# One chunk of every seventeenth group gathered row by row by SyncE in two graph passes

## The chip, the cores and the metric

The kernel runs on one core of one Trainium2 chip. The metric is device time in microseconds (us); the median of three runs before is 9730.03 us. Its engines are TensorE (PE; its weight loads are PEld), VectorE (DVE), ScalarE (ACT), GpSimd (POOL) and SyncE (SP); a q behind a name is the engine's sequencer.

## What is computed

Four graph layers over one graph of 6250 nodes and 100000 edges (`dst` sorted), each followed by a layer norm. Layers 1 and 2 concern us: per edge a score is made from a row of the source node and a row of the destination node, the scores are normalised by a softmax over the edges of each destination, and the weighted source rows are summed per destination.

```python
# layer 1 (relational attention, 8 heads)
kt = einsum('nhi,thij->tnhj', k, relation_att)[edge_type, src]
e = (q[dst] * kt).sum(-1) * relation_pri[edge_type] * scale
a = softmax over the edges of each dst (e)
vt = einsum('nhi,thij->tnhj', v, relation_msg)[edge_type, src]
agg = segment_sum(a[..., None] * vt, dst)
# layer 2 (additive attention, 4 heads, with self loops)
e = leaky_relu(x_l[src] + x_r[dst], 0.2)
logits = einsum('ehc,hc->eh', e, att)
out = segment_sum(softmax(logits)[:, :, None] * x_l[src], dst)
```

## The kernel before, in words

Edges are sorted by destination into 832 chunks of 128 edges (one edge to a partition), `G = 4` chunks to a group, `GROUPS = 208`. `read_order` (L734) reads the sorted list from DRAM as rows of 104 partitions, turns it on TensorE and writes the SBUF lists of indices `by_dst.other` (source node) and `by_dst.typed` (type times `NPD`, plus source node): one column of 128 indices for a chunk. SP then stores the segment breaks, and the block ends when the store has landed.

`softmax_pass` (L1361) runs once for each of layers 1, 2 and 3; the change touches the first two calls (L3266, L3283). It has no scheduler: the work of every engine is written out in one order, and semaphores link them.

- POOL (L1495 to L1507) gathers the source rows: one indirect DMA a chunk, 128 rows of 1024 bytes in layer 1 (`related`) or 528 bytes in layer 2 (`left_table`), into `rows`, a ring of `ring = lag + 1` groups. Here `lag = wg + 6`, and a window is `wg` groups: 4 in layer 1, 8 in layer 2. From the ring's second round on, group n waits for `weighed >= n - ring + 1`, that is, until DVE has weighed group n - ring. So POOL may fill group n once DVE has finished its turn n - 1.
- DVE (L1698 on) takes turns n = 0, 1, 2, ... In turn n it marks the one-hots of group n (helper line L140), pairs group n - 2 with its destination rows (L1788 in layer 1, L1791 in layer 2), reduces the pair to scores (L1814), weighs group n - lag (L1877) and adds the sums of group n - lag - 2 into `total` (L1694). In some turns of each window it also takes the steps of the running maximum: L1760, L1798 to L1845, and the waits for `small`, which PE makes (L1765, L1831). It is first in, first out: a wait in turn n holds all of this back.
- PE turns the one-hots (L1569), fetches destination rows by matmul (L1582; in layer 2 it also adds the gathered rows, and so waits for them there) and makes the sums (L1600, L1610).
- SP (L1474 to L1494) loads the breaks at the start of a pass (`brk`, L1479: 32 DMAs in layer 1, 64 in layer 2), and has nothing more until the pass ends (in layer 1 `reload` at L1492).

`load_blocks` (L129) loads several numbers from one partition of SBUF into registers of an engine, by one TENSOR_LOAD.

```python
pool.wait_ge(weighed if at else scored, n - ring + 1 + (NBLK // G if ringed else 0))
nc.gpsimd.indirect_dma_start(rows[:, s, g, :], None, table, ...).then_inc(got[s], 16)
dve.wait_ge(got[t % ring], (t // ring + 1) * 16 * G)
```

Of the kernel before, what the change touches and what calls it, by code (L numbers as in the profile page):

```python
# [48 lines left out]
AFTER = NSLOT - E  # L49
assert TU * QU == CU and RING * G == 64 and NBLK < (RING - 2) * G  # L50
# [683 lines left out]
def read_order(nc, k, table, o, breaks, fields, name, stack=None, shared=None):  # L734


    with ExitStack() as own:
# [7 lines left out]
        end = sb("end", [1, P], BF16)  # L745
        outs = [out for _, out in fields] + [o.begins]
# [614 lines left out]
def softmax_pass(nc, k, o, index, table, row, head, values_at, spread, att, peaks, total, reload, loops, wg, name, beside=(),  # L1361
                 ringed=False):
# [21 lines left out]
    with ExitStack() as ctx:  # L1384
# [73 lines left out]
        kept = sem("kept")  # L1458
        block = ctx.enter_context(nc.Block())
# [15 lines left out]
        def _(sp):  # L1475
# [11 lines left out]
            if beside:  # L1487
                sp.wait_ge(kept, 16 * len(beside))
            if reload is not None:
# [6 lines left out]
        def _(pool):  # L1496
            for n in range(GU if ringed else GROUPS):
# [5 lines left out]
                for g in range(G):  # L1503
# [52 lines left out]
        def _(pe):  # L1556
# [4 lines left out]
            for n in range(slots):  # L1561
# [10 lines left out]
                if 0 <= t < GROUPS:  # L1572
# [6 lines left out]
                    if att is not None:  # L1579
                        pe.wait_ge(got[t % ring], (t // ring + 1) * 16 * G)  # L1580
# [81 lines left out]
        def _(dve):  # L1662
# [33 lines left out]
            for n in range(slots + 1):  # L1696
# [3 lines left out]
                if n >= GROUPS + 2:  # L1700
                    add_sums(n - lag - 2)
                if n < GROUPS:
# [65 lines left out]
                if 0 <= t < GROUPS:  # L1768
# [6 lines left out]
                    else:  # L1775
                        dve.wait_ge(got[t % ring], (t // ring + 1) * 16 * G)
# [1356 lines left out]
def graph_network(nc, a, out):  # L3133
    k = Shared()
    k.semaphores = []
    with ExitStack() as ctx:
# [27 lines left out]
        by_src.free = sb("src_free", [1, 2 * P], I32)  # L3164
        by_dst.typed = sb("dst_typed", [P, CH + SPARE], I32)
# [11 lines left out]
        with ExitStack() as sort:  # L3177
# [51 lines left out]
            with unblocked as dense:  # L3229
                def tmp(name, shape, dt=F32):  # L3230
# [31 lines left out]
                       [(1, by_dst.other), (2, by_dst.typed), (0, by_dst.place)], "dst_read")  # L3262
            free_semaphores(nc, k)
        with ExitStack() as layer:
            total = layer.enter_context(nc.sbuf_tensor("l1_total", [P, NBLK - 1 + G, D + HEADS1], F32))
            softmax_pass(nc, k, by_dst, by_dst.typed, related.rearrange("t n f -> (t n) f"), 2 * D, D // HEADS1, D,  # L3266
                         k.x, None, False, total, (k.x[:], x_home), None, 4, "l1_pass")
# [6 lines left out]
        with ExitStack() as layer:  # L3274
            def tmp(name, shape, dt=F32):
# [8 lines left out]
                         None, (left, loop_scores, k.x[:], bias2[:]), 8, "l2_pass")  # L3284
# [47 lines left out]
```

## Time and profile before

| | us |
|---|---|
| median of 3 runs (lowest, highest) | 9730.03 (9727.62, 9735.21) |
| the profiled execution, its own time | 9737.26 |
| its span | 9735.5 |
| pass of layer 1, first gather to last | 5188.4 to 6251.5 |
| pass of layer 2, first gather to last | 6429.9 to 7481.0 |
| busy: PE, DVE, ACT, POOL | 6374.2, 6539.5, 2118.1, 6993.0 |

Times within the span count from its start. An engine's busy time leaves out its sequencer's work, which a view of SP or of a line shows as SPq, DVEq and so on. Idle time is put down to what ended it; "issue" is idle time in which the engine waited for nothing that the profile shows.

### The profile page before, as it was taken

What the parts mean: (1) busy time and instruction counts of PE and PEld (TensorE: products, weight loads), DVE (VectorE), ACT (ScalarE), POOL (GpSimd) and SP (SyncE); (2) the same over time, 40 slices, a digit from 0 to 9 for tenths busy, and PEclk for the clock granted to TensorE, in tenths of its full rate; (3) what the DMA queues carried; (4) which work ended last, traced back from release to release, by engine and by line L of the source; (5) the groups of instructions that cost most, each with busy time, mean ns of one, the idle gap of its engine ahead of it and who ended that gap; (6) DMA issues with size and microseconds to landing.
All of it is one profiled execution on the core that took longest, in us unless ns stands there. A gap on an engine that the chain in (4) does not pass through costs nothing. (4 is left out here: it accounts for less than half of the span.)

```text
span 9735.5 us, 171552 instructions
## 1 busy us (share of the span) xinstructions
PE 6374.2 (65%) x37681; PEld 5551.4 (57%) x37682; DVE 6539.5 (67%) x22695; ACT 2118.1 (22%) x6216; POOL 6993.0 (72%) x7418
## 2 busy tenths in 40 slices
PE   6777655547666577639404666767776688876666
PEld 5666544436655566634204666556675578766665
DVE  7555566668777777736305888877777666667777
ACT  5222100001111111112101222232222222223333
POOL 7777777767777777777776777547775577767775
PEclk7555555556666655569756888889999665667777
DMA  0000012122212212234303333222222322223333
GB/s 25 2 2 2 18 53 52 53 61 53 53 53 55 57 53 53 53 77 146 100 2 86 104 104 104 87 47 55 55 55 55 100 54 54 54 72 108 108 108 97
DMA packets 436037, 614.74 MB, mean 63 GB/s; under 512 B 176561, under 2 KB 312069, under 8 KB 435109
## 3 DMA queue, kind: packets, MB, share of 16 engines
q0 software_dynamic: 257024, 486.93, 19.6%
q1 hardware_dynamic: 178305, 119.49, 4.3%
q8 instruction: 183, 3.00, 0.1%
q10 hardware_dynamic: 292, 3.41, 0.1%
q14 instruction: 233, 1.91, 0.1%
HBM read 520.17 MB, written 89.19 MB: 63 GB/s over the span
## 5 line engine op out<-in xcount | busy, mean ns | idle before, releaser
L1179 PE MATMUL hop_sums<-hop_rows,hop_weighted 128*128 x4992 | 1152.1, 403 | 1053.2 <-SPq L1315 674.4
L1128 POOL DMA_INDIRECT hop_rows<-hops,k_src_gather x1568 | 1483.3, 946 | 486.8 <-issue 477.6
L1179 PEld LDWEIGHTS hop_sums<-hop_rows,hop_weighted 128*128 128x128 f32 x4992 | 989.6, 295 | 1158.8 <-issue 1158.7
L1505 POOL DMA_INDIRECT l_pass_rows<-left_table,k_dst_other x832 | 796.2, 957 | 433.2 <-issue 244.6
L1505 POOL DMA_INDIRECT l_pass_rows<-related,k_dst_typed x832 | 788.6, 948 | 308.6 <-issue 238.7
L1505 POOL DMA_INDIRECT l_pass_rows<-key_table,k_src_gather x784 | 744.3, 949 | 365.9 <-issue 234.8
L2000 POOL DMA_INDIRECT l_weigh_rows<-row_table,l_weigh_ring x832 | 790.0, 949 | 297.9 <-issue 213.1
L728 POOL DMA_INDIRECT src_sorted<-src_scatter_records,src_scatter_places x784 | 753.1, 961 | 260.4 <-issue 188.2
L1355 POOL DMA_INDIRECT dst_sorted<-rec,dst_places x768 | 752.8, 980 | 237.2 <-issue 237.2
L1128 POOL DMA_INDIRECT hop_rows<-in_x,k_src_gather x784 | 742.4, 947 | 249.0 <-issue 238.7
L1213 DVE TENSOR_SCALAR hop_weighted<-k_numbers,k_src_place,src_weight 128x128 f32<-128x128 f32 x2496 | 850.1, 403 | 15.7 <-issue 8.7
L1521 ACT CAST l_pass_onehot_t<-l_pass_turned 128x512 f32<-128x512 bf16 x624 | 365.7, 586 | 2158.6 <-PE l_pass_turned L1569 2110.8
L1600 PE MATMUL l_pass_sums<-l_pass_zero 128*128 128x272 bf16 (+1 forms) x1210 | 235.7, 279 | 465.2 <-DVE l_total L1694 322.0
L1582 PE MATMUL l_pass_own<-l_right,l_pass_onehot_t 128*128 x1664 | 359.0, 299 | 257.7 <-DMA l_pass_rows<-left_table,k_dst_other 243.8
L1610 PE MATMUL l_pass_sums<-l_pass_terms,l_pass_onehot_f 128*128 128x136 f32 x3232 | 513.1, 308 | 1.1 <-DVE l_pass_terms L1877 1.1
L664 PE MATMUL src_scatter_nexts<-src_scatter_next_sb,src_scatter_oh_lo_t 128*128 128x50 f32 x1568 | 494.2, 425 | 0.0
L1106 ACT COPY hop_next_sb<-hop_next_ps 128x50 f32<-128x50 f32 x784 | 158.1, 202 | 1522.6 <-PE hop_next_ps L1151 1516.5
L1610 PEld LDWEIGHTS l_pass_sums<-l_pass_terms,l_pass_onehot_f 128*128 128x128 f32 x3232 | 472.1, 217 | 26.3 <-issue 3.2
L2018 PE MATMUL l_weigh_own<-l_keys,l_weigh_onehot_t 128*128 x1672 | 321.5, 352 | 229.9 <-ACT l_weigh_onehot_t L1970 229.9
L1814 DVE TENSOR_REDUCE l_pass_scores<-l_pass_pair 128x32 f32<-128x512 f32 (+1 forms) x624 | 426.2, 683 | 14.5
L1582 PEld LDWEIGHTS l_pass_own<-l_right,l_pass_onehot_t 128*128 128x128 f32 x1664 | 267.1, 202 | 289.7 <-issue 289.7
L2018 PEld LDWEIGHTS l_weigh_own<-l_keys,l_weigh_onehot_t 128*128 128x128 f32 x1672 | 272.4, 247 | 274.6 <-issue 274.6
(477 smaller groups left out, 17048.9 us busy)
## 6 DMA issues: line engine op xcount, KB each, us to landing
related<-l_tables_rows SPq DMA_DIRECT2D x50, 1024.0 KB, 4.5
hop_rows<-hops,k_src_gather POOLq DMA_INDIRECT x1568
l_pass_rows<-related,k_dst_typed POOLq DMA_INDIRECT x832
l_pass_rows<-left_table,k_dst_other POOLq DMA_INDIRECT x832
l_weigh_rows<-row_table,l_weigh_ring POOLq DMA_INDIRECT x832
src_sorted<-src_scatter_records,src_scatter_places POOLq DMA_INDIRECT x784, 2.1
hop_rows<-in_x,k_src_gather POOLq DMA_INDIRECT x784, 2.5
dst_sorted<-rec,dst_places POOLq DMA_INDIRECT x784
```

The costliest lines, as they stand in the source:

```text
L664: nc.tensor.matmul(nexts[:, b, g, 0:HIS], oh_lo_t[:, b, g, :], next_sb[:, g % 2, :], start=True, stop=True).then_inc(looked, 1)
L728: nc.gpsimd.indirect_dma_start(table, bass.IndirectOffsetOnAxis(ap=places[:, s, g:g + 1], axis=0), records[:, s, g, :], None).then_inc(sen ...
L1128: nc.gpsimd.indirect_dma_start(rows[:, s * G + g, :], None, table_in, bass.IndirectOffsetOnAxis(ap=o.gather[:, c:c + 1], axis=0),).then_in ...
L1179: last = nc.tensor.matmul(sums[:, b, g, :], weighted[:, s % SLOTS, g, :], rows[:, bass.ds(slots[g], 1), :], start=True, stop=True)
L1213: last = nc.vector.tensor_scalar(weighted[:, s, g, :], k.numbers, o.place[:, c], o.weight[:, c], ALU.is_equal, ALU.mult)
L1355: nc.gpsimd.indirect_dma_start(table, bass.IndirectOffsetOnAxis(ap=places[:, c:c + 1], axis=0), rec[:, c, :], None).then_inc(sent[c % SLOT ...
L1505: nc.gpsimd.indirect_dma_start(rows[:, s, g, :], None, table, bass.IndirectOffsetOnAxis(ap=index[:, c:c + 1], axis=0),).then_inc(got[s], 16)
L1582: last = nc.tensor.matmul(own[:, b, g, :], onehot_t[:, b, g, :], spread[:, bass.ds(blocks[g], 1), :], start=True, stop=(att is None))
L1610: last = nc.tensor.matmul(into[:, bass.ds(within[g], 1), 0:width], onehot_f[:, m % 2, g, :], term, start=False, stop=False, skip_group_che ...
L1814: nc.vector.tensor_reduce(mine, pair[:, b, :, :, :].rearrange("p (s t) h f -> p s t h f", t=per), AX.X, ALU.add).then_inc(scored, 1)
L2000: nc.gpsimd.indirect_dma_start(rows[:, s, g, :], None, table, bass.IndirectOffsetOnAxis(ap=ring[:, s, g:g + 1], axis=0),).then_inc(got[s], 16)
L2018: last = nc.tensor.matmul(own[:, b, g, :], onehot_t[:, b, g, :], spread[:, bass.ds(blocks[g], 1), :], start=True, stop=True)
```

## The change

`side_groups` are the groups 20, 37, 54, ..., 207 (12 of them). In layers 1 and 2 POOL gathers only three chunks of such a group. The fourth is gathered by SP, which reads the 128 indices from a DRAM copy of the list (`row_home`) into one partition, loads 8 at a time into registers, and issues a DMA of one row for each into `side`, a tile of two buffers. In turn n of a side group DVE waits for the 128 rows and copies them to their place in `rows`. `read_order` makes the DRAM copies: POOL computes the two lists from the loaded rows, SP stores them, and the end of the block waits for these stores too.

```diff
+FIRST_SIDE, SIDE_STEP = 20, 17
+AT_ONCE = 8
...
@@ read_order, SP and POOL
             sp.dma_start(breaks[0:NSLOT].rearrange("(q p e) -> p q e", q=QT, e=P), breaks_sb[:]).then_inc(stored, 16)
-            sp.wait_ge(stored, 32)
+            sp.wait_ge(homed, 4)
+            for tile, home in ((other_i, other_home), (typed_i, typed_home)):
+                sp.dma_start(home.rearrange("(q p) e -> p q e", q=QT), tile[:]).then_inc(stored, 16)
+            sp.wait_ge(stored, 64)
+
+        @block.gpsimd
+        def _(pool):
+            for h in range(2):
+                here = slice(h * half, (h + 1) * half)
+                pool.wait_ge(loaded[h], 16)
+                nc.gpsimd.tensor_copy(other_i[:, here, :], by_edge[:, here, :, 1]).then_inc(homed, 1)
+                nc.gpsimd.tensor_scalar(first_row[:, here, :], by_edge[:, here, :, 2], float(NPD), None, ALU.mult).then_inc(first_ok, 1)
+                pool.wait_ge(first_ok, h + 1)
+                nc.gpsimd.tensor_tensor(first_row[:, here, :], first_row[:, here, :], by_edge[:, here, :, 1],
+                                        ALU.add).then_inc(row_ok, 1)
+                pool.wait_ge(row_ok, h + 1)
+                nc.gpsimd.tensor_copy(typed_i[:, here, :], first_row[:, here, :]).then_inc(homed, 1)
@@ softmax_pass, SP, behind the loads of brk
+            def list_side(j):
+                c = side_groups[j] * G + G - 1
+                sp.dma_start(side_list[:, j % 2, :], row_home[c:c + 1, :]).then_inc(side_listed[j % 2], 16)
+
+            for j in range(2 if side_groups else 0):
+                list_side(j)
+            for j, n in enumerate(side_groups):
+                b = j % 2
+                sp.wait_ge(side_listed[b], 16 * (j // 2 + 1))
+                if j >= 2:
+
+                    sp.wait_ge(side_in, j - 1)
+                for first in range(0, P, AT_ONCE):
+                    nodes = load_blocks(nc, sp.engine, side_list[:, b, first:first + AT_ONCE], AT_ONCE, table.shape[0] - 1)
+                    for e, node in enumerate(nodes):
+                        sp.dma_start(side[first + e:first + e + 1, b, :], table[bass.ds(node, 1), :]).then_inc(side_got[b], 16)
+                if j + 2 < len(side_groups):
+                    list_side(j + 2)
@@ softmax_pass, POOL
-                for g in range(G):
+                for g in range(G - 1 if n in side_groups else G):
@@ softmax_pass, PE and, with the same lines, DVE
-                        pe.wait_ge(got[t % ring], (t // ring + 1) * 16 * G)
+                        pe.wait_ge(got[t % ring], gathered(t))
+                        if t in side_groups:
+                            pe.wait_ge(side_in, side_groups.index(t) + 1)
@@ softmax_pass, DVE, turn n, ahead of its one-hots
+                if n in side_groups:
+                    j = side_groups.index(n)
+
+                    dve.wait_ge(side_got[j % 2], (j // 2 + 1) * 16 * P)
+                    if n >= ring:
+                        dve.wait_ge(weighed, n - ring + 1)
+                    nc.vector.tensor_copy(rows[:, n % ring, G - 1, :], side[:, j % 2, :]).then_inc(side_in, 1)
```

On SP, in the pass of layer 1, this stands before between the loads of `brk` and the reload of `k.x`:

```order
L1479 DMA l_pass_brk<-dst_breaks 8x48x129 x16
L1492 DMA k_x<-x_home 128x6400
```

and in the changed kernel, whose lines it numbers (the first rows; `l_pass_side_list` is the list of 128 indices, `l_pass_side` the tile of rows):

```order
L1515 DMA l_pass_brk<-dst_breaks 8x48x129 x16
L1528 DMA l_pass_side_list<-dst_typed_home 1x128 x2
L133 TENSOR_LOAD l_pass_side_list
L1541 ISA
L1541 DMA l_pass_side<-related 1x256
L1541 ISA
L1541 DMA l_pass_side<-related 1x256
```

Eight such pairs follow each TENSOR_LOAD and sixteen TENSOR_LOADs make a chunk: 1536 one-row DMAs a pass, behind the loads of `brk`, where SP had nothing.

In an earlier block of SP stand DMAs whose address comes from a register; the sequencer's instructions of this one appear in the trace as FUSED_REGOPS, MOVE and DMA_DIRECT2D:

```order
L2436 ISA
L2436 DMA related<-l_tables_rows 128x8x256
```

So the ISA of a row is the FUSED_REGOPS, and the MOVE comes with the DMA; neither moved.

On POOL, from `read_order` to the end of the pass of layer 2, before:

```order
L1505 DMA l_pass_rows<-related,k_dst_typed 128x256 x832
L1384 UNCONDITIONAL_BRANCH
L74 ISA
L1495 UNCONDITIONAL_BRANCH
L1505 DMA l_pass_rows<-left_table,k_dst_other 128x132 x832
```

and in the changed kernel:

```order
L789 CAST dst_read_other_i<-dst_read_lst 104x512
L790 TENSOR_SCALAR dst_read_first_row<-dst_read_lst 104x512
L792 TENSOR_TENSOR dst_read_first_row<-dst_read_first_row,dst_read_lst 104x512
L795 CAST dst_read_typed_i<-dst_read_first_row 104x512
...
L1560 DMA l_pass_rows<-related,k_dst_typed 128x256 x820
...
L1560 DMA l_pass_rows<-left_table,k_dst_other 128x132 x820
```

POOL has four operations more for each half in `read_order`, and 12 gathers less in each pass.

## Rows read from the trace of the kernel before

**Rows 1.** The page's group: count, busy us, mean ns, idle before, its releasers

```profile
L1505 POOL DMA_INDIRECT l_pass_rows<-related,k_dst_typed x832 | 788.6, 948 | 308.6 <-issue 238.7
```

**Rows 2.** Busy us (x instructions): PE, PEld, DVE, ACT, POOL; granted clock, DMA, GB/s

```profile
5300.00:5600.00 300.00, 210.78 (x1467) 189.66 (x1467) 240.30 (x599) 77.02 (x203) 222.42 (x236) 0.83 0.36 104
6540.00:6840.00 300.00, 224.33 (x1888) 206.16 (x1887) 226.28 (x486) 89.22 (x257) 226.83 (x241) 0.98 0.25 55
```

**Rows 3.** Layer 1's waits (us, times, longest): DVE, whole pass; POOL, 5300:5600

```profile
DVE l_pass_breaks_in L1831 <- PE l_pass_small L1658: 70.5, 49, 1.4
DVE l_pass_picked L1765 <- PE l_pass_small L1643: 59.3, 39, 2.3
DVE l_pass_pair L1788 <- DMA l_pass_rows<-related,k_dst_typed: 20.2, 8, 7.0
...
POOL l_pass_rows L1505 <- DVE l_pass_terms L1877: 11.8, 24, 0.8
```

**Rows 4.** Waits in layer 2's pass: PE's, then POOL's

```profile
PE l_pass_own L1582 <- DMA l_pass_rows<-left_table,k_dst_other: 243.8, 165, 7.9
...
POOL l_pass_rows L1505 <- DVE l_pass_terms L1877: 11.2, 31, 2.1
```

**Rows 5.** DVE's one-hots, first and last start: turns 0-20, 0-207, by layer

```profile
L140 DVE TENSOR_TENSOR l_pass_onehot<-l_pass_numbers,k_dst_place x21: 656/679/690, 5189.0 to 5289.5; 128x512 bf16<-128x512 f32 x21
...
L140 DVE TENSOR_TENSOR l_pass_onehot<-l_pass_numbers,k_dst_place x208: 656/680/690, 5189.0 to 6246.8; 128x512 bf16<-128x512 f32 x104
...
L140 DVE TENSOR_TENSOR l_pass_onehot<-l_pass_numbers,k_dst_place x21: 653/681/691, 6430.5 to 6536.3; 128x512 bf16<-128x512 f32 x21
...
L140 DVE TENSOR_TENSOR l_pass_onehot<-l_pass_numbers,k_dst_place x208: 653/681/691, 6430.5 to 7474.5; 128x512 bf16<-128x512 f32 x104
```

**Rows 6.** Timeline of SP's queue (start, us): end of read_order; loads of brk

```profile
5183.68 0.30 SPq L770 DMA_DIRECT2D dst_breaks<-dst_read_breaks_sb  x1
5187.74 51.95 SPq L1479 DMA_DIRECT2D l_pass_brk<-dst_breaks  x32
...
6429.23 29.05 SPq L1479 DMA_DIRECT2D l_pass_brk<-dst_breaks  x64
```

**Rows 7.** SP's DMAs one behind another: of 16 partitions, of one, of 8

```profile
4375.81 3.67 SPq L2379 DMA_DIRECT2D l_att<-in_L_gnn_relation_att  x8
...
4769.72 0.41 SPq L972 DMA_DIRECT2D src_breaks<-src_breaks_end  x1
...
L1479 SPq DMA_DIRECT2D l_pass_brk<-dst_breaks x10: 264/301/363, 5187.7 to 5190.9; - x10
```

**Rows 8.** SP's DMAs addressed by a register: ns min/median/max, starts

```profile
L2239 SPq MOVE poly_z<-hops x3: 29/29/38, 4273.5 to 4274.6; - x3
L2239 SPq DMA_DIRECT2D poly_z<-hops x3: 372/475/479, 4273.6 to 4274.6; - x3
L2239 SPq FUSED_REGOPS  x1: 46/46/46, 4273.4 to 4273.4; - x1
```

**Rows 9.** Loads into registers: SP's of one number, DVE's of four

```profile
L1318 SPq TENSOR_LOAD <-k_src_free x540: 262/267/465, 1217.1 to 4126.8; - x180
L1318 SPq FUSED_REGOPS  x540: 147/147/190, 1217.6 to 4127.1; - x180
...
L131 DVEq TENSOR_LOAD <-k_src_slot x208: 340/347/357, 7610.0 to 8592.2; - x104
```

**Rows 10.** DVE's weighing of 512 elements and copy of 128, in layer 1

```profile
L1877 DVE TENSOR_TENSOR l_pass_terms<-l_pass_rows,l_pass_numbers 128x512 f32<-128x512 f32 x200 | 134.0, 670 | 1.7
L1873 DVE COPY l_pass_numbers<-l_pass_weights 128x128 f32<-128x128 f32 x50 | 19.1, 383 | 0.0
```

**Rows 11.** DMA issues: count, size, us to landing; a group of POOL

```profile
hops<-hop_total SPq DMA_DIRECT2D x21, 448.0 KB, 5.0
l_att<-in_L_gnn_relation_att SPq DMA_DIRECT2D x8, 8.0 KB, 1.8
...
L347 POOL TENSOR_SCALAR src_count_oh_lo<-k_count,src_keys 128x128 bf16<-128x128 f32 x196 | 114.2, 625 | 13.8 <-PEq L383 11.8 <-PE src_count_total L394 0.7
```

More of the change, by code:

```diff
@@ L731, in _, with read_order @@
                 pool.wait_ge(sent[s], 64 * (groups // SLOTS))
-def read_order(nc, k, table, o, breaks, fields, name, stack=None, shared=None):
+def read_order(nc, k, table, o, breaks, fields, other_home, typed_home, name, stack=None, shared=None):
     with ExitStack() as own:
@@ L745, in read_order @@
         end = sb("end", [1, P], BF16)
+        other_i = sb("other_i", [TQ, QT, P], I32)
+        typed_i = sb("typed_i", [TQ, QT, P], I32)
+        first_row = sb("first_row", [TQ, QT, P])
+        homed = sem("homed")
+        first_ok = sem("first_ok")
+        row_ok = sem("row_ok")
         outs = [out for _, out in fields] + [o.begins]
@@ L1361, in softmax_pass @@
 def softmax_pass(nc, k, o, index, table, row, head, values_at, spread, att, peaks, total, reload, loops, wg, name, beside=(),
-                 ringed=False):
+                 ringed=False, row_home=None):
     heads = D // head
@@ L1458, in softmax_pass, with gathered @@
         kept = sem("kept")
+        side_groups = range(FIRST_SIDE, GROUPS, SIDE_STEP) if row_home is not None else ()
+        if row_home is not None:
+            side = sb("side", [P, 2, row])
+            side_list = sb("side_list", [1, 2, P], I32)
+            side_listed = [sem(f"side_listed{b}") for b in range(2)]
+            side_got = [sem(f"side_got{b}") for b in range(2)]
+            side_in = sem("side_in")
+        def gathered(n):
+            return sum(16 * (G - 1 if before in side_groups else G) for before in range(n % ring, n + 1, ring))
         block = ctx.enter_context(nc.Block())
@@ L1775, in _ @@
                     else:
-                        dve.wait_ge(got[t % ring], (t // ring + 1) * 16 * G)
+                        dve.wait_ge(got[t % ring], gathered(t))
+                        if t in side_groups:
+                            dve.wait_ge(side_in, side_groups.index(t) + 1)
                     dve.wait_ge(spread_ok, t + 1)
@@ L3164, in graph_network @@
         by_src.free = sb("src_free", [1, 2 * P], I32)
+        by_dst.other_home, by_dst.typed_home = dram("dst_other_home", [CH, P], I32), dram("dst_typed_home", [CH, P], I32)
         by_dst.typed = sb("dst_typed", [P, CH + SPARE], I32)
@@ L3261, in graph_network @@
             read_order(nc, k, by_dst.sorted, by_dst, by_dst.breaks,
-                       [(1, by_dst.other), (2, by_dst.typed), (0, by_dst.place)], "dst_read")
+                       [(1, by_dst.other), (2, by_dst.typed), (0, by_dst.place)], by_dst.other_home, by_dst.typed_home, "dst_read")
             free_semaphores(nc, k)
@@ L3266, in graph_network @@
             softmax_pass(nc, k, by_dst, by_dst.typed, related.rearrange("t n f -> (t n) f"), 2 * D, D // HEADS1, D,
-                         k.x, None, False, total, (k.x[:], x_home), None, 4, "l1_pass")
+                         k.x, None, False, total, (k.x[:], x_home), None, 4, "l1_pass", row_home=by_dst.typed_home)
             relation_output(nc, k, total, a["L1_gnn_w_basis_a"], a["L1_gnn_loop_weight"], a["L1_gnn_bias"], mix,
@@ L3283, in graph_network @@
             softmax_pass(nc, k, by_dst, by_dst.other, left_table, D + HEADS2, D // HEADS2, 0, right, att_row[:], True, total,
-                         None, (left, loop_scores, k.x[:], bias2[:]), 8, "l2_pass")
+                         None, (left, loop_scores, k.x[:], bias2[:]), 8, "l2_pass", row_home=by_dst.other_home)
             attention_output(nc, k, total, loop_scores, left_table, "l2_out")
```

## Prediction

> **What bounds the kernel now.** I read the page's groups first, then the two passes by stretch, then the waits, because the share of busy time does not tell whether a pass is paced by POOL. A gather costs POOL 0.948 us and 238.7/832 = 0.287 us of issue [rows 1], so four cost 4.94 us and a saved one is worth at most 1.24 us. The two passes then differ.
>
> In **layer 1** DVE is busy 240 of 300 us and POOL 222 us [rows 2]. The waits decide: over the whole pass DVE waited for gathered rows 8 times, 20.2 us, against 70.5 and 59.3 us for PE's small products alone, while POOL waited 11.8 us in 300 for DVE [rows 3]. The turns run at (6246.8 - 5289.5)/187 = 5.12 us [rows 5], longer than POOL's 4.94. So the chain between DVE and PE bounds this pass and POOL has a little room: a gather less is worth nothing, and whatever holds DVE is lost.
>
> In **layer 2** PE waited for gathered rows 165 times, 243.8 us, and POOL for DVE only 11.2 us in the whole pass [rows 4]. The turns take (7474.5 - 6536.3)/187 = 5.017 us [rows 5], which is 4 x 1.254. POOL bounds it, and a saved gather is worth 1.25 us.
>
> SP is free in both passes once the loads of brk are issued, at 5187.7 + 52.0 = 5239.7 and 6429.2 + 29.1 = 6458.3 [rows 6]. DVE starts the one-hots of turn 20, the first side group, at 5289.5 and 6536.3 [rows 5]. SP has 50 and 78 us for its first chunk.
>
> **The change, part by part.** Everything hangs on T, SP's time for one chunk of 128 rows.
>
> *One row* is a FUSED_REGOPS of 46 ns, a MOVE of 29 ns [rows 8], the DMA, and three gaps. Eight DMAs took 3.67 us [rows 7], 0.46 each; less an instruction of about 0.42, a gap is 0.04 us. For the DMA from one partition the nearest row is the one-partition store, 0.41 us; the bounds are 0.30, a DMA of 8 partitions [rows 7], and 0.475, an addressed DMA right behind another [rows 8]. The same rows 8 show 0.372 for one that came after a pause, and here some 0.19 us of other work stands between two DMAs, so I take 0.39: 0.046 + 0.029 + 0.39 + 0.12 = 0.585 us. With 0.41 it is 0.605, with the bounds 0.495 and 0.67.
>
> *One load of eight numbers* is between SP's load of one, 0.267, and a little over DVE's of four, 0.347; I take 0.35, plus 0.10 because the register operation behind it takes 0.147 and not 0.046 [rows 8, 9], plus a gap: 0.49. Sixteen are 7.8 us, and the next list's DMA 0.4.
>
> **T = 128 x 0.585 + 8.2 = 83 us**; with the store's 0.41 it is 85.5, with the bounds 72 and 94. The skill speaks against this price: the Trainium skill, "DMA: Bandwidth & Descriptors", section "Latency and other measured facts", gives a floor of about 600 ns for a tensor load. SP's own loads here took 267 ns [rows 9], so the measurement decides; by the page's figure T would be an estimated 87 us, and the whole change would cost some 83 us.
>
> *The first side chunk.* Two lists are issued and landed in 0.9 + 1.8 us [rows 11], so SP starts at 5242.4 and 6461.0. The rows are there at 5242.4 + 83 + 1.8 = 5327.2 and 6545.8.
> - Layer 1: DVE stands 5327.2 - 5289.5 = 37.7 us in turn 20. Behind that wait are its one-hots, pairs, weighing and sums, PE and ACT wait for those, and POOL may run only to group 20. The chain has no slack to catch up: **+37.7 us**.
> - Layer 2: 9.5 us late. while DVE stands in turn 20, POOL may go on to the end of group 20, some 7.5 us of work that is not lost, and the chain, in which PE waits 1.5 us a turn for rows, catches up afterwards. **+2 us**.
>
> *The other eleven.* A side group comes every 17 turns. In layer 1 that is 87.0 us, more than T, so no more stalls. In layer 2 it is 85.3 - 1.25 = 84.0 us, one more than T.
>
> *DVE's copy* of 256 elements lies between a copy of 128 (0.38, part of it start-up that overlaps) and the weighing of 512 (0.67) [rows 10]. I take 0.3 on the chain: 12 x 0.3 = **+3.6 us** in layer 1 (0 to 8), nothing in layer 2, where the rows come later anyway.
>
> *Gathers saved.* 12 in layer 1: **0**, hidden by the chain. If DVE's chain were faster they would show. 12 in layer 2: 12 x 1.25 = **-15 us**.
>
> *read_order.* SP's store of the breaks was issued at 5183.7 and the next block's first DMA at 5187.7 [rows 6]. Now two stores of 416 KB follow. A store of 448 KB lands in 5.0 us where one lands of l_att takes 1.8 [rows 11]; against the small store in its place that is about +3, plus 0.9 of issue. POOL's eight operations begin with the loads and lie beside DVE's; each has 512 elements to a partition. The nearest group has 128 in 625 ns [rows 11]: at 2.5 us each they would end some 10 us behind DVE, while at 0.6 us they are hidden. I take **+5 us** (3 to 14).
>
> Sum: 37.7 + 3.6 + 2 - 15 + 5 = +33 us, on the profiled execution's own 9737.3 (span 9735.5 and 1.8 around it): 9770.6. That execution was 7.2 us above the median of the runs, 9730.0, so I predict **9763 us**.
>
> **How the sum moves with T.** While T is under 84, each microsecond costs one in layer 1's first stall and next to nothing in layer 2. Above it, SP's pace rules layer 2: its twelfth chunk lands at 6462.8 + 12 T against turn 207 at 7474.5 [rows 5]. Above 87.3 it rules layer 1 as well: 5244.2 + 12 T against 6246.8. So T = 85.5 gives +41.3 + 3.6 in layer 1 (with the stall at 40.2, +44), +14 in layer 2, +5: +63. T = 94 gives 125 + 116 + 5 = +246. T = 72 gives 26.7 + 3.6 - 15 + 5 = +20.
>
> **The rivals.**
> - *SP becomes the bound.* T lies above 84, and DVE waits at every side group of layer 2, above 87.3 in layer 1 too. For it: the one-partition store's own 0.41 already gives T = 85.5, and an addressed DMA right behind another took 0.475. Against it: the pause between DMAs. Time: 9793 at T = 85.5, 9833 at 88, up to 9976 at 94. Chance 0.30.
> - *The DMA of one row is issued in much less time* (the other side: not slower). A DMA of 8 partitions took 0.30 where one of 16 took 0.42 [rows 7]; carried on to one partition this is some 0.19, a row 0.385, T = 57. The first chunk then lands at 5301, a stall of 12, layer 2 has none, and the sum is 12 + 3.6 - 15 + 5 = +5: 9736, no change. It decides where T is under 71, a DMA under 0.29. Against it: the one-partition store took 0.41 and not 0.19. The Trainium skill, "DMA: Bandwidth & Descriptors", section "Why a DMA increments its semaphore by 16 and not by 1", has a copy use as many engines as divide its slowest dimension, one here, while the sequencer writes the rest of the increment; by that rule the issue could fall with the engines, and the store's row speaks against it. Chance 0.12.
> - *POOL's relief counts in layer 1 too*, with fast issue: POOL's margin there is only 0.18 us a turn. The savings of both layers would be 30 us against a stall of 12, with copies and stores: -9 us or a little below, 9720. Chance 0.03.
> - *The landings do not overlap.* If each row's 1.8 us were paid in turn, T would be over 230 us and each pass some 1800 us longer. Eight DMAs were issued in 3.67 us, each with 1.8 us to land, so they do overlap. Chance 0.01.
>
> **How the numbers follow.** About 0.2%, 19.5 us, is what a measurement of this kernel can tell from no change. The forecast, T from 72 to 84, has 0.54 and its own range is 9750 to 9775. SP as the bound has 0.30, fast issue 0.12, the last two together 0.04. The range reaches down to 9742 and up to 9850, T between 88 and 89, where about one in ten is left out on either side. Faster by more than 0.2%: 0.02. Within: the fast issue, the lower edge of the forecast, 0.13. Slower: 0.85.
>
> **What would show it.** In the changed profile: SP's one-row DMAs start 0.585 us apart (0.50 to 0.67), a first list of 128 takes 83 us; DVE stands once in layer 1, before turn 20, for about 38 us and ends on a side DMA; turn 207 of layer 1 comes some 41 us later relative to the pass's start, and the stretch from turn 21 to 207 is as long as before; in layer 2 that stretch is 13 us shorter and POOL stays without gaps; the first gather of layer 1 comes 5 us later. The prediction is wrong if DVE waits at the later side groups, if layer 1's stretch behind turn 20 shrinks, or if the rows start under 0.5 us apart.

## The result and the profile after

The changed kernel takes 9751.0 us, the median of 20 runs (9742.25 to 9765.94), against 9730.2 us before (20 runs, 9722.06 to 9744.32): a ratio of 1.0021, 95% interval 1.0014 to 1.0028, or 20.8 us more. The profiled execution took 9759.4 us, with a span of 9757.7. Of the executions told of below one, at 10558 us, stands far above the others of its kernel and is left out of that kernel's median.

SP's timeline at the first pass of the changed kernel (start us, us, engine, line, operation, count) answers to [rows 6]:

```profile
5172.04 0.30 SPq L778 DMA_DIRECT2D dst_breaks<-dst_read_breaks_sb  x1
5172.38 0.53 SPq L781 DMA_DIRECT2D dst_other_home<-dst_read_other_i  x1
5172.95 1.14 SPq L781 DMA_DIRECT2D dst_typed_home<-dst_read_typed_i  x1
5180.16 52.84 SPq L1515 DMA_DIRECT2D l_pass_brk<-dst_breaks  x32
5233.04 0.65 SPq L1528 DMA_DIRECT2D l_pass_side_list<-dst_typed_home  x2
5240.79 65.90 SPq L1541 DMA_DIRECT2D l_pass_side<-related  x128
5306.73 0.24 SPq L1528 DMA_DIRECT2D l_pass_side_list<-dst_typed_home  x1
5307.96 66.09 SPq L1541 DMA_DIRECT2D l_pass_side<-related  x128
```

The loads of brk end at 5233.0, as in [rows 6] 53 us into the pass. The two lists are asked for in 0.65 us, but the first row goes out only at 5240.8. From then on a chunk takes 5307.96 - 5240.79 = **67.2 us**, the T of the prediction, and not 83. The rows of the side DMA's line and of the register load in the changed kernel say why (ns min/median/max, first and last start), to be read beside [rows 7 to 9]:

```profile
L1541 SPq FUSED_REGOPS  x3072: 37/37/43, 5240.6 to 7383.7; - x192
L1541 SPq MOVE l_pass_side<-related x1536: 29/29/37, 5240.7 to 6159.2; - x192
L1541 SPq DMA_DIRECT2D l_pass_side<-related x1536: 224/225/288, 5240.8 to 6159.2; - x192
...
L133 SPq TENSOR_LOAD <-l_pass_side_list x384: 685/780/960, 5239.9 to 7380.0; - x192
```

A one-row DMA took 225 ns and the load of eight numbers 780 ns. The DMA took the same 225 ns for the rows of 528 bytes:

```profile
L1541 SPq DMA_DIRECT2D l_pass_side<-left_table x1536: 224/225/278, 6481.5 to 7383.9; - x192
```

Within the eight rows behind one load the DMAs start 0.41 us apart; with its share of the loads a row takes 67.2/128 = 0.525 us.

DVE's waits in layer 1's pass of the changed kernel (us in all, times, longest), against [rows 3]:

```profile
DVE l_pass_breaks_in L1897 <- PE l_pass_small L1715: 68.9, 49, 1.4
DVE l_pass_picked L1829 <- PE l_pass_small L1700: 55.7, 39, 2.1
DVE l_pass_rows L1765 <- DMA l_pass_side<-related: 26.9, 1, 26.9
DVE l_pass_pair L1854 <- DMA l_pass_rows<-related,k_dst_typed: 20.9, 8, 7.4
```

One wait is new: 26.9 us, once, for a side DMA. PE's products and the first gathers hold DVE as long as before. DVE's one-hots in the changed kernel (ns min/median/max, first and last start), against [rows 5], for layer 1 up to turn 20 and up to turn 207, then the same for layer 2:

```profile
L142 DVE TENSOR_TENSOR l_pass_onehot<-l_pass_numbers,k_dst_place x21: 655/681/691, 5181.5 to 5308.1; 128x512 bf16<-128x512 f32 x21
...
L142 DVE TENSOR_TENSOR l_pass_onehot<-l_pass_numbers,k_dst_place x208: 655/681/693, 5181.5 to 6265.3; 128x512 bf16<-128x512 f32 x104
...
L142 DVE TENSOR_TENSOR l_pass_onehot<-l_pass_numbers,k_dst_place x21: 653/681/692, 6448.9 to 6555.8; 128x512 bf16<-128x512 f32 x21
...
L142 DVE TENSOR_TENSOR l_pass_onehot<-l_pass_numbers,k_dst_place x208: 653/682/692, 6448.9 to 7483.0; 128x512 bf16<-128x512 f32 x104
```

In layer 1 turn 20 comes 126.6 us after turn 0 instead of 100.5, and the 187 turns behind it take 6265.3 - 5308.1 = 957.2 us, before 6246.8 - 5289.5 = 957.3: nothing lost and nothing won in them. That this isn't a gain from POOL and a loss from the copies that cancel, the waits behind turn 20 of layer 1 tell. In the kernel before (5290 to 6247) and in the changed kernel (5309 to 6265) no wait of DVE there is for a gathered row. These are the two longest of each kernel, and between them PE's only row in the kernel before (us in all, times, longest):

```profile
DVE l_pass_breaks_in L1831 <- PE l_pass_small L1658: 66.2, 46, 1.4
DVE l_pass_picked L1765 <- PE l_pass_small L1643: 52.6, 35, 1.7
PE l_pass_sums L1600 <- DVE l_total L1694: 288.6, 141, 3.1
DVE l_pass_breaks_in L1897 <- PE l_pass_small L1715: 64.7, 46, 1.4
DVE l_pass_picked L1829 <- PE l_pass_small L1700: 50.9, 35, 1.6
```

Nobody waited for POOL, so POOL's relief had nothing to shorten. DVE's two waits for PE fell by 3.2 us in all, and its eleven copies took 11 x 0.28 = 3.1: the copies went into time that DVE had waited anyway.

In layer 2 the 187 turns behind turn 20 take 927.2 instead of 938.2 us. In read_order, DVE's small comparison of four elements (L800 before, L824 after) shows something that no row ahead of the prediction did. DVE's timeline there (start us, us) in the kernel before:

```profile
5177.53 0.17 DVE L800 TENSOR_TENSOR dst_read_starts<-dst_read_lst,dst_read_before 104x4 f32<-104x4 f32 x1 [3.58 <-DMA dst_read_before<-dst_sorted]
5181.04 0.16 DVE L800 TENSOR_TENSOR dst_read_starts<-dst_read_lst,dst_read_before 104x4 f32<-104x4 f32 x1
```

And DVE's and POOL's timelines in the changed kernel:

```profile
5162.85 1.10 DVE L824 TENSOR_TENSOR dst_read_starts<-dst_read_lst,dst_read_before 104x4 f32<-104x4 f32 x1 [3.55 <-DMA dst_read_before<-dst_sorted]
5166.00 1.18 DVE L842 TENSOR_SCALAR dst_read_breaks_sb<-dst_read_starts 104x512 bf16<-104x512 f32 x1
5167.10 1.04 DVE L821 TENSOR_TENSOR dst_read_starts<-dst_read_lst 104x508 f32<-104x508 f32 x1
5168.07 1.49 DVE L824 TENSOR_TENSOR dst_read_starts<-dst_read_lst,dst_read_before 104x4 f32<-104x4 f32 x1
5162.42 1.51 POOL L792 TENSOR_TENSOR dst_read_first_row<-dst_read_first_row,dst_read_lst 104x512 f32<-104x512 f32 x1
5165.79 1.99 POOL L790 TENSOR_SCALAR dst_read_first_row<-dst_read_lst 104x512 f32<-104x512 f32 x1
5167.86 1.67 POOL L792 TENSOR_TENSOR dst_read_first_row<-dst_read_first_row,dst_read_lst 104x512 f32<-104x512 f32 x1
```

The small comparison took 1.10 and 1.49 us where it had taken 0.17 and 0.16. Each time POOL had begun its own addition of 512 elements a moment earlier, and DVE's end falls on POOL's: 5163.95 and 5163.93, 5169.56 and 5169.53. DVE's conversion of the breaks (5166.00) took 1.18 us where the same line in the kernel before took 0.42, beside POOL's multiplication (5165.79 to 5167.78), but does not end with it. The Trainium skill, "SBUF — State Buffer", section "Who interferes with whom", has a DVE instruction with two SBUF inputs contend with a GpSimd instruction that reads SBUF, where the one that started first keeps the shared port to its end. The two additions agree with that: the ends fall together to 0.03 us. A third pair does not: DVE's comparison of 508 elements, which reads two inputs from SBUF as well, began at 5167.10 inside POOL's multiplication and took 1.04 us, as in the kernel before (1.05); why is open. The prediction had left this rule out, though it speaks against the change.

The stages of the two profiled executions, each from the first DMA of its stage to that of the next, in us:

| stage | before | after | change |
|---|---|---|---|
| read_order | 22.0 | 29.0 | +7.0 |
| layer 1, pass and output | 1241.5 | 1267.4 | +25.9 |
| layer 2, pass and output | 1179.2 | 1166.9 | -12.3 |
| sum of the three | 2442.7 | 2463.3 | +20.6 |

The sum is closer to the measured 20.8 us than the method is good for: in the eleven variants below the two differ by 1 to 8 us, so this closeness is luck. Of layer 2's -12.3 us, -9.9 lie between turns 0 and 207; the other 2.4 lie behind turn 207, where this kernel took 131.5 us and the kernel before 133.9 in this profile and 132.3 in another, so most of them may be chance. The stages that the change leaves alone moved too, by -14.7 us ahead of read_order (5165.8 to 5151.1) and +16.1 us from layer 3 on (2127.1 to 2143.2); what that is worth is told with the experiments.

### The profile page after: what moved, and what is told of

Read it like the earlier page. It is cut to its first block and busy times, and to the rows that moved or that the text cites. A ratio compares the mean times of both kernels' runs of the same rounds, so it can differ in the third digit from the quotient of the medians.

```text
span 9757.7 us, 181266 instructions
## 1 busy us (share of the span) xinstructions
PE 6418.2 (66%) x37681; PEld 5595.5 (57%) x37682; DVE 6548.5 (67%) x22719; ACT 2116.2 (22%) x6216; POOL 6963.6 (71%) x7402
## 5 line engine op out<-in xcount | busy, mean ns | idle before, releaser
L1177 PE MATMUL hop_nexts<-hop_next_sb,hop_oh_lo_t 128*128 128x50 f32 x1568 | 432.8, 374 | 0.0
```

What stands on the lines that cost most here:

```text
L1177: nc.tensor.matmul(nexts[:, b, g, 0:HIS], oh_lo_t[:, b, g, :], next_sb[:, g % 2, :], start=True, stop=True).then_inc(looked, 1)
```

## The experiments

The table has the ratio to the kernel before (with its interval), and from each profile the length of read_order, the stretch from turn 0 to turn 20 and from 20 to 207 in layer 1, and from turn 0 to 207 in layer 2, in us.

| kernel | us | ratio | read_order | layer 1: 0 to 20 | 20 to 207 | layer 2: 0 to 207 |
|---|---|---|---|---|---|---|
| before | 9730.2 | 1 | 22.0 | 100.5 | 957.2 | 1044.0 |
| the change | 9751.0 | 1.0021 (1.0014 to 1.0028) | 29.0 | 126.6 | 957.2 | 1034.1 |
| lists made, not used | 9747.6 | 1.0015 (1.0005 to 1.0025) | 28.9 | 101.9 | 957.4 | 1043.8 |
| layer 1 only | 9767.0 | 1.0036 (1.0022 to 1.0050) | 29.1 | 122.6 | 958.5 | 1043.8 |
| layer 2 only | 9727.0 | 0.9992 (0.9983 to 1.0002) | 29.0 | 101.9 | 956.9 | 1032.8 |
| first side group 37 | 9732.1 | 1.0001 (0.9992 to 1.0011) | 29.0 | 100.0 | 957.3 | 1033.9 |
| no row DMAs | 9730.0 | 0.9996 (0.9986 to 1.0005) | 28.8 | 102.4 | 956.4 | 1032.5 |
| rows ahead of brk | 9751.0 | 1.0019 (1.0009 to 1.0028) | 29.1 | 105.9 | 970.3 | 1037.2 |
| four numbers a load | 9761.1 | 1.0028 (1.0018 to 1.0038) | 29.1 | 131.9 | 958.1 | 1030.8 |
| layer 2, one in 14 | 9727.7 | 0.9995 (0.9986 to 1.0004) | 25.0 | 102.5 | 956.9 | 1037.0 |
| before, once more | 9722.6 (one run) | | 21.8 | 101.3 | 956.9 | 1043.8 |
| POOL's operations only | 9739.6 | 1.0006 (0.9996 to 1.0015) | 25.2 | 100.9 | 957.0 | 1044.1 |
| lists ahead of brk | 9742.4 | 1.0012 (1.0002 to 1.0021) | 29.1 | 119.3 | 958.4 | 1032.7 |
| layer 2, list stored late | 9712.4 | 0.9979 (0.9970 to 0.9988) | 22.6 | 102.8 | 957.5 | 1026.6 |

The ratios of the variants are to the kernel before as it was run beside them, in three batches with medians of 9730.3, 9733.1 and 9730.6 us. All edits are made to the changed kernel.

**Lists made, not used.** Neither pass gets `row_home`.

```diff
-                         k.x, None, False, total, (k.x[:], x_home), None, 4, "l1_pass", row_home=by_dst.typed_home)
+                         k.x, None, False, total, (k.x[:], x_home), None, 4, "l1_pass")
-                         None, (left, loop_scores, k.x[:], bias2[:]), 8, "l2_pass", row_home=by_dst.other_home)
+                         None, (left, loop_scores, k.x[:], bias2[:]), 8, "l2_pass")
```

> Only the two lists are made and stored in read_order; both passes are as before, with 832 gathers. If the sum is right part by part, read_order's end (from the breaks' store to the next block's first DMA) goes from 4.06 to 8.1 us, as in the changed kernel, the passes keep 101.8 us to turn 20 and 957.2 us from turn 20 to 207 in layer 1, and the kernel takes about 4 us more than before. If POOL's eight operations or the stores disturb more than that, the first pass starts later or runs slower: 10 us or more.

The passes are as before within 2 us, and read_order takes 28.9. My 8.1 us from the breaks' store on were right (5172.04 to 5180.16 in the changed kernel); what I had not seen is that the store itself came 3 us later. By the ratio the kernel takes 14.6 us more, with an interval of 5 to 24 us; the 7 us of the stage lie inside the interval, at its low end.

**Layer 1 only, layer 2 only.** Each keeps `row_home` in one of the two calls and drops it from the other, for layer 1 only:

```diff
-                         None, (left, loop_scores, k.x[:], bias2[:]), 8, "l2_pass", row_home=by_dst.other_home)
+                         None, (left, loop_scores, k.x[:], bias2[:]), 8, "l2_pass")
```

> SP's rows in layer 1 alone. Theory (the chain of DVE and PE bounds layer 1, POOL's saved gathers are hidden): turn 20 comes 26 us later, turns 20 to 207 take 957 us as before although POOL has 12 gathers less, and the kernel takes 26 + 4 = 30 us more than before. Rival (POOL's relief counts in layer 1, and something else gives it back): turns 20 to 207 fall by up to 15 us, and the kernel takes 15 to 20 us more.

> SP's rows in layer 2 alone. Theory (POOL bounds layer 2): the pass is 12 us shorter, turn 20 comes 1 us later and turns 20 to 207 take 927 us instead of 938; with the 4 us of read_order the kernel takes 8 us less than before. Rival (the 12 us of the changed kernel's profile were chance): the pass stays within 3 us, and the kernel takes 4 us more.

In layer 1 alone turn 20 comes 22 us later and the turns behind it take 958.5 us: POOL's twelve gathers fewer show nowhere. The stall was 22.5 us, 4.4 shorter than in the changed kernel, mostly because the loads of brk took 49.0 us to issue here and 52.8 there. In layer 2 alone the pass is 11.2 us shorter. The parts add up: the rival for layer 1 falls, and layer 2's gain is there by itself.

**First side group 37.**

```diff
-FIRST_SIDE, SIDE_STEP = 20, 17
+FIRST_SIDE, SIDE_STEP = 37, 17
```

> The first side group is 37 instead of 20, so 11 side groups a pass. SP's first chunk is there at 128 us of layer 1's pass, and turn 37 comes at 190. Theory (the loss is the first stall alone): no stall, turns 0 to 207 of layer 1 in 1059 us as before, layer 2 shorter by 11 us, read_order 4 more: 7 us less than before, 28 less than the changed kernel. Rival (SP's stream of small DMAs or DVE's copies cost layer 1 something throughout): layer 1 stays 5 us or more above 1059.

One number takes away the whole loss in layer 1: no stall, 1057.3 us from turn 0 to 207 against 1057.7 before, with eleven chunks gathered by SP and copied by DVE. Since POOL's relief is worth nothing there (no wait for a gathered row behind turn 20), SP's stream of small DMAs and DVE's copies cost this pass nothing. The kernel came to 9732 us, 19 below the changed one.

**No row DMAs.** SP issues no rows (nor their register loads) and DVE copies a tile of zeros, so the side chunks' rows are left out of the computation.

```diff
-                for first in range(0, P, AT_ONCE):
-                    nodes = load_blocks(...)
-                    for e, node in enumerate(nodes):
-                        sp.dma_start(side[...], table[bass.ds(node, 1), :]).then_inc(side_got[b], 16)
...
+                    if j == 0:
+                        nc.vector.memset(side[:], 0.0).then_inc(side_got[0], 1)
```

> SP's 3072 row DMAs are left out and DVE copies a cleared tile in their place, so the side chunks' rows are zeros; POOL has its 820 gathers and DVE its copies. Theory: this is the most the change can give. Layer 1: no stall and no gain, 1059 us to turn 207; layer 2: 12 to 15 us less; with read_order's 4 us the kernel takes 8 to 11 us less than before. Rival (SP's DMAs slow the others): more than that comes back, 15 us or over.

Layer 2 takes 1032.5 us, and in kernels that issue the same rows there 1034.1 (the change), 1032.8 (layer 2 only), 1032.7 (lists ahead of brk) and 1030.8 (four numbers a load). So no cost of SP's 1536 DMAs shows above the 3 us by which these differ. In layer 1 it is 1058.7 us even though POOL is relieved and nothing is late. That pass has nothing to gain from POOL.

**Rows ahead of brk.** The first chunk's rows go between the two batches of loads.

```diff
             for n, here in enumerate((slice(0, batch), slice(batch, windows))):
+                if n and side_groups:
+                    gather_side(0)
```

> SP asks for the lists first and issues the first side chunk between the two batches of loads of brk, of which the second serves turns from 64 (layer 1) on. Theory (the first chunk is late for the 53 us of loads ahead of it and the 7 us that its list took to land behind them): the chunk is there at about 75 us in layer 1, turn 20 comes at 102 as before, the kernel takes 8 us less than before with all 24 side chunks. Rival (the first chunk's late arrival has another cause, or the second batch of brk now comes late): turn 20 at over 110, or a wait of DVE for brk near turn 64.

I had misread `batch`: it counts windows, 16 // wg = 4 of them in layer 1, so the second batch is needed in turn 4 x 4 + 4 = 20 as well. The rival came true at an earlier place than I had put it, and DVE's wait in this kernel's pass (us in all, times, longest) names it:

```profile
DVE l_pass_low L1817 <- DMA l_pass_brk<-dst_breaks: 13.7, 1, 13.7
```

The rows did arrive in time, the loads of brk did not. The window of SP's time ahead of turn 20 holds one of the two.

**Four numbers a load.**

```diff
-AT_ONCE = 8
+AT_ONCE = 4
```

> Four numbers to a load instead of eight: 32 loads a chunk. If a load on SP costs by the number (0.27 for one, 0.78 for eight: 0.073 each), one of four takes 0.49 us, a chunk's loads 15.6 instead of 12.5 us, T 69 to 70 instead of 67.2 us, the stall in layer 1 2 to 3 us longer. If eight cost 0.78 because of the DMAs in flight and not for their count, one of four takes about as long, loads 25 us, T 79 us, stall 12 us longer.

The register load of this kernel (ns min/median/max, first and last start):

```profile
L133 SPq TENSOR_LOAD <-l_pass_side_list x768: 457/557/759, 5240.1 to 7390.5; - x192
```

A load of four takes 557 ns, one of eight 780, one of a single number 267 [rows 9]; T became 73.6 us (rows of one chunk from 5240.83, of the next from 5314.45). That is between the two theories: most of the cost goes with the numbers, some 60 to 100 ns for each one more, but four cost 70 ns more than the straight line between one and eight.

**Layer 2, one in 14.** No `row_home` in layer 1, the first chunk ahead of the second batch of brk, `FIRST_SIDE, SIDE_STEP = 16, 14`, and only layer 2's list made.

```diff
-FIRST_SIDE, SIDE_STEP = 20, 17
+FIRST_SIDE, SIDE_STEP = 16, 14
...
-            for tile, home in ((other_i, other_home), (typed_i, typed_home)):
+            for tile, home in ((other_i, other_home),):
...
             for n, here in enumerate((slice(0, batch), slice(batch, windows))):
+                if n and side_groups:
+                    gather_side(0)
```

> Side chunks in layer 2 alone, one in fourteen groups from group 16 on (14 of them), the first chunk's rows ahead of the second batch of loads of brk, and only layer 2's list made. T of 67 us fits 14 turns of 5.0 less 1.25 = 69 us. Theory: layer 2 shorter by 14 x 1.0 to 1.25 = 14 to 17 us, layer 1 as before, read_order 2 to 3 us longer: 12 to 14 us less than before. Rival (SP's pace binds at this density): DVE waits at side groups and the pass is less than 10 us shorter.

DVE's waits in this kernel's layer 2 have one row for the side chunks (us in all, times, longest):

```profile
DVE l_pass_rows L1764 <- DMA l_pass_side<-left_table: 4.7, 1, 4.7
```

The pass was 7 us shorter, though 14 gathers are gone. The timelines of SP, DVE and POOL in this kernel place that wait (start us, us):

```profile
6434.43 66.19 SPq L1519 DMA_DIRECT2D l_pass_side<-left_table  x128
6500.96 17.60 SPq L1530 DMA_DIRECT2D l_pass_brk<-dst_breaks  x32
6519.55 66.19 SPq L1519 DMA_DIRECT2D l_pass_side<-left_table  x128
6513.39 0.23 DVE L1764 COPY l_pass_rows<-l_pass_side 128x132 f32<-128x132 f32 x1
6586.89 0.23 DVE L1764 COPY l_pass_rows<-l_pass_side 128x132 f32<-128x132 f32 x1 [4.70 <-DMA l_pass_side<-left_table]
6590.78 0.94 POOL L1559 DMA_INDIRECT l_pass_rows<-left_table,k_dst_other  x1 [3.36 <-DVE l_pass_terms L1942]
```

The first chunk was copied in turn 16 without a wait. The second, needed in turn 30, came 4.7 us late: SP had the second batch of loads of brk to issue, 17.6 us, between the first two chunks. POOL, which paces this pass, then stood 3.4 us for DVE. In the whole pass POOL waited 21.7 us for DVE, in the last kernel below, which has its rows behind all of brk, 12.0; the two passes differ by 10.4 us. So the rival came true in part: SP's pace did bind, at one side group and through brk. Before that, turns 0 to 20 took 109.3 us where the changed kernel has 106.9, and what held those is open.

**Before, once more.** The kernel before, unchanged.

> The kernel before, profiled once more, to see which stages move by themselves. The stretch from the pass of layer 3 to the end took 2127 us in its first profile and 2126 to 2150 in the others, the stretch ahead of read_order 5166 and 5151 to 5157. If these differences are chance, this profile shows values inside those ranges and not again the first ones, with the passes of layers 1 and 2 at 1241.5 and 1179.2 us within 2; if the added code or its memory shifts them, they repeat at 2127 and 5166.

From layer 3 to the end it took 2125.6 us, 1.5 less than in the first profile of it, while read_order began at 5153.9 and not at 5165.8. So the stretch ahead moves by chance by 12 us. The stretch behind looks like more than chance: 2127.1 and 2125.6 for the kernel before, 2125.5 to 2150.2 for the changed kernel and the eleven variants, with a mean of 2139. But two profiles of the kernel before are few, and the times speak against a lasting 12 us: over these twelve kernels the difference by the ratio lies on average only 1.2 us above the sum of the three stages, from 6.8 below to 7.8 above. Whether anything lengthens the stretch is open.

**POOL's operations only.** As the first experiment, without SP's stores of the lists.

```diff
-            sp.wait_ge(homed, 4)
-            for tile, home in ((other_i, other_home), (typed_i, typed_home)):
-                sp.dma_start(home.rearrange("(q p) e -> p q e", q=QT), tile[:]).then_inc(stored, 16)
-            sp.wait_ge(stored, 64)
+            sp.wait_ge(stored, 32)
```

> POOL's eight operations in read_order alone: SP doesn't store the lists, the passes are as before. From the first load to the next block's first DMA it was 22.0 us before and is 29.0 in the changed kernel. Theory: 4 of the 7 us are the wait for the stores, 3 are POOL's operations beside DVE's, which slow DVE; so 25 us here. Rival: all 7 hang on the stores; then 22 us.

read_order took 25.2 us, and DVE's small comparisons 1.14 and 1.50 us, by DVE's timeline in this kernel (start us, us):

```profile
5169.21 1.14 DVE L821 TENSOR_TENSOR dst_read_starts<-dst_read_lst,dst_read_before 104x4 f32<-104x4 f32 x1 [3.52 <-DMA dst_read_before<-dst_sorted]
5174.44 1.50 DVE L821 TENSOR_TENSOR dst_read_starts<-dst_read_lst,dst_read_before 104x4 f32<-104x4 f32 x1
```

So 3.2 of the 7 us come from POOL's operations beside DVE's (2.3 in the two comparisons, 0.75 in the first conversion of the breaks, which took 1.17 us again), and the other 3.8 from the wait for the stores. The last kernel below, whose POOL makes one list and has no additions, shows it from the other side (DVE and POOL, start us, us):

```profile
5166.51 0.90 DVE L811 TENSOR_TENSOR dst_read_starts<-dst_read_lst,dst_read_before 104x4 f32<-104x4 f32 x1 [3.47 <-DMA dst_read_before<-dst_sorted]
5166.30 1.08 POOL L782 CAST other_i<-dst_read_lst 104x512 int32<-104x512 f32 x1 [2.28 <-DMA dst_read_lst<-dst_sorted]
5170.75 0.15 DVE L811 TENSOR_TENSOR dst_read_starts<-dst_read_lst,dst_read_before 104x4 f32<-104x4 f32 x1
```

The comparison beside POOL's conversion ends with it (5167.41 and 5167.38); the second, with POOL idle, takes 0.15 us as in the kernel before.

**Lists ahead of brk.** Both first lists are asked for before the loads.

```diff
+            for j in range(2 if side_groups else 0):
+                list_side(j)
             for n, here in enumerate((slice(0, batch), slice(batch, windows))):
```

> The first two lists are asked for ahead of the loads of brk; all else as in the changed kernel. Theory (the list took 6.4 us to land because it stood behind the loads of brk, which now cost nothing): SP starts its rows 6 us earlier, the stall in turn 20 of layer 1 falls from 26.9 to about 21 us, the stretch to turn 207 from 1085 to 1079. Rival (loads of brk still in flight slow the rows themselves, not the list): the rows start earlier but land as late, and the stall stays at 27.

SP's timeline in this kernel, and DVE's wait for the side DMA (us in all, times, longest):

```profile
5180.69 0.52 SPq L1514 DMA_DIRECT2D l_pass_side_list<-dst_typed_home  x2
5181.26 49.45 SPq L1521 DMA_DIRECT2D l_pass_brk<-dst_breaks  x32
5231.80 68.10 SPq L1541 DMA_DIRECT2D l_pass_side<-related  x128
...
DVE l_pass_rows L1765 <- DMA l_pass_side<-related: 19.0, 1, 19.0
```

The first row goes out 1.1 us after the last load of brk and no longer 7.8 us after, and DVE's wait falls to 19.0 us, where 21 was expected. The list had waited behind the loads. The rows themselves took 2 us longer than in the changed kernel (68.1 for 65.9), so the rival has that much.

**Layer 2, list stored late.**

```diff
-FIRST_SIDE, SIDE_STEP = 20, 17
+FIRST_SIDE, SIDE_STEP = 20, 14
@@ read_order: POOL makes other_i alone, a tile that lives to the end of layer 1
-            for tile, home in ((other_i, other_home), (typed_i, typed_home)):
-                sp.dma_start(home.rearrange("(q p) e -> p q e", q=QT), tile[:]).then_inc(stored, 16)
@@ the call of layer 1's pass: SP stores it there as `beside`
-                         k.x, None, False, total, (k.x[:], x_home), None, 4, "l1_pass", row_home=by_dst.typed_home)
+                         k.x, None, False, total, (k.x[:], x_home), None, 4, "l1_pass",
+                         [(other_i[:], by_dst.other_home.rearrange("(q p) e -> p q e", q=QT), False)])
```

and the lists are asked for ahead of brk. Layer 1 keeps its gathers on POOL.

> What the other runs point to: side chunks in layer 2 alone, one in fourteen groups from 20 (14 of them), its list asked for ahead of brk, and the list's copy stored by SP during layer 1's pass, when nothing waits for it; POOL makes that list alone. Theory: layer 1's pass as before (1241 to 1244), read_order 22 to 24 us, layer 2's stretch 13 to 15 us shorter than 1179: the kernel takes 11 to 14 us less than before. Rival (POOL's gathers are not what binds at this density, or the stores disturb layer 1): under 8 us less.

DVE's one-hots up to turn 207 of layer 2 in this kernel, and SP's rows of its first two chunks (start us, us):

```profile
L142 DVE TENSOR_TENSOR l_pass_onehot<-l_pass_numbers,k_dst_place x208: 652/681/690, 6422.9 to 7449.6; 128x512 bf16<-128x512 f32 x104
...
6452.13 66.02 SPq L1528 DMA_DIRECT2D l_pass_side<-left_table  x128
6519.43 65.85 SPq L1528 DMA_DIRECT2D l_pass_side<-left_table  x128
```

Layer 2 takes 7449.6 - 6422.9 = 1026.7 us from turn 0 to 207, 17.4 less than before for 14 gathers, 1.24 each. A chunk takes 67.3 us of SP and the side groups stand 14 turns, 69 us, apart. Its three stages come to 13.7 us less than before (read_order 22.6, the passes with their outputs 1244.2 and 1162.3), inside the 11 to 14 of the theory. The kernel takes 9712.4 us, 0.9979 (0.9970 to 0.9988) of the one before, which is 12 to 29 us less: it beats both, and with both lists first no side chunk came late.

## Why the prediction was right, and where it was not

The direction, the place of the loss and the split between the layers came as predicted; the time lies 12 us below the forecast because T was too large. By its own signs the prediction was wrong on the price of a row: it named starts under 0.5 us apart as such a sign, and within a load of eight they lie 0.41 apart. T = 67.2 lies outside the forecast's 72 to 84 and, with a DMA of 0.225, under the 71 and 0.29 at which it gave the case to fast issue. With T = 67.2 its own stall would be 21.9 us and its sum 33.3 - 15.8 - 2 = +15.5, or some 9746 us. That the time still came within 12 us of 9763 is in part luck: the list's late landing put 4.6 us back and read_order 2 more.

- **Layer 1 is bound by DVE and PE, a saved gather is worth nothing.** Right: 957.2 us behind turn 20 before and after, and no gain with the rows left out or the first group moved, and behind turn 20 no wait for a gathered row to shorten. That answers the rival of POOL's relief.
- **Layer 2 is bound by POOL.** Right. The 11 side groups behind turn 20 gave 11.0 us, 1.0 each instead of 1.25; the same stretch gave 12.1 in the kernel with layer 2 only and 13.3 with four numbers a load, so a gather was worth 1.0 to 1.2, and with one in fourteen 1.24. The first chunk's +2 us did not come, because with T = 67.2 the chunk was there in time: DVE waited for no side DMA in layer 2. Turn 20 came at 106.9 instead of 105.8, but so it did in the kernel without side chunks in layer 2 (layer 1 only, 106.9).
- **T = 83 us.** This is the step that failed; it was 67.2. The DMA of one row was taken at 0.39 us and took 0.225, 128 x 0.165 = 21 us less. The load of eight was taken at 0.35 and took 0.78, 16 x 0.43 = 7 us more. FUSED_REGOPS took 37 ns instead of 46, behind a load too, where I had added 0.10 us sixteen times: together 3 us less. That makes 83 - 21 + 7 - 3 = 66 us, measured 67.2. The 21 and the 7 are errors of opposite sign, and only part of the first shows in T. The error was to price a one-partition load by the one-partition store (0.41 us) against the trend of the rows of 8 and 16 partitions. The rival of fast issue had 0.19 from that trend, and is nearer; its T of 57 missed the price of the loads. The Trainium skill, "DMA: Bandwidth & Descriptors", section "Why a DMA increments its semaphore by 16 and not by 1", by which such a copy uses one engine, fits the cheaper issue: from 5241 to 5300 the queue moved 227 packets for 114 row DMAs, two each, which is the row and one semaphore write, as that section has it for one engine; that page's floor of 600 ns for a tensor load (section "Latency and other measured facts"), which I had set aside, lies between the load of four here (557) and that of eight (780), and does not fit one of a single number (267): the count of numbers decides.
- **The start of the first chunk.** 1.8 us for the lists to land were 6.4, behind the loads of brk. With T = 67.2 and this, my own sum for the stall gives 5242.4 + 4.6 + 67.2 + 1.8 - 5289.5 = 26.5 us; measured, 26.9.
- **DVE's copies, +3.6 us.** They took 0.28 us each in layer 1, where I took 0.3, and cost nothing: eleven of them lie in the 957.2 us, and DVE's waits for PE are shorter by as much. No run has the copies without POOL's relief or the other way round, so this rests on the waits.
- **read_order, +5 us.** It was 7.0, because POOL's operations slowed DVE by 3.2 us where I had taken them as hidden.
- **The sum.** By the stages 25.9 - 12.3 + 7.0 = 20.6 us, measured 20.8; I had 41.3 - 13 + 5 = 33. (Where the prediction writes +41.3 + 3.6 for layer 1 at T = 85.5, the 3.6 stands twice; its +44 beside it is the right figure. And its 1.5 us that PE waits "a turn" in layer 2 is the mean of 165 waits; over 208 turns it is 1.2.) SP's pace bound nothing: 67.2 us is under the 84 and 87.3 us at which it would have.

## What to carry to other kernels

Moving work off an engine pays only in the passes which that engine bounds: read who waited for whom before counting its busy time, pass by pass. When a slow helper takes over a part, its first delivery decides first: give it a first deadline that it can meet, and put its own request ahead of the bulk loads on its queue. Count those loads for the second delivery too, if they are split around the first. And ask of an idle engine's new work whose port or unit it shares; here POOL's eight operations cost DVE 3 us of a chain although nothing waited for them.

## What was not expected of the hardware

- A DMA of one row into one partition took SP 225 ns to issue, whether the row had 528 or 1024 bytes, one of 8 partitions 301 and one of 16 about 420 [rows 7]; yet the store from one partition [rows 7] had taken 0.41 us.
- A load of registers on SP cost 267 ns for one number, 557 for four and 780 for eight, where DVE's load of four cost 347 [rows 9].
- A list of 512 bytes took 6.4 us to land behind 32 loads of brk, and stood ready at once when it was asked for ahead of them.
- Beside POOL's tensor operations, DVE's comparison of four elements took 0.9 to 1.5 us instead of 0.17, up to the end of POOL's addition or conversion; beside POOL's multiplication one of 508 elements took no longer than before.
